# Gathers on GpSimd: one wait a block for the landing of the 15 fixed gathers, in place of waits for PE's lookups and second FFN layer

## The reference, cut to what matters

```python
n = x.shape[0]
xp = (x @ W).reshape(n, H, C)                      # H = 4 heads, C = 64
a_src = jnp.einsum('nhc,hc->nh', xp, att_src)
a_dst = jnp.einsum('nhc,hc->nh', xp, att_dst)
alpha = leaky_relu(a_src[src] + a_dst[dst], 0.2)   # one per edge and head
ex = jnp.exp(alpha - amax[dst])
w = ex / segment_sum(ex, dst)[dst]
msg = xp[src] * w[..., None]                       # the rows that are gathered
agg = segment_sum(msg, dst)
x = x + elu(agg.reshape(n, H * C) + bias)
...
h = gelu(sel @ w1 + b1); y = (h @ w2 + b2) * w_sel # FFN, of layernorm(x)
```

## Time and profile before

| | |
|---|---|
| time, median of 3 runs | 2211.67 us (2209.64 to 2214.61) |
| span of the profiled execution | 2573.5 us |
| POOL busy | 1554.5 us (60%), 1,626 instructions |
| of it the gathers (L692) | 1512.9 us, 1,563 of 968 ns on average |
| PE busy | 1981.2 us (77%) |
| DVE busy | 1581.4 us (61%) |
| ACT busy | 744.5 us (29%) |
| DMA engines, mean over the span | 143 GB/s |

### The profile page before, as it was taken

How to read it: one execution, slowest core, us unless ns; L and a number is a source line. 1 busy time by engine, 2 the same in 40 slices (tenths; PEclk the granted TensorE clock), 3 DMA queues, 4 the chain that set the end, 5 groups by cost and what they waited for, 6 DMA issues and landing times.

```text
span 2573.5 us, 29095 instructions
## 1 busy us (share of the span) xinstructions
PE 1981.2 (77%) x9511; PEld 1633.8 (63%) x9512; DVE 1581.4 (61%) x3510; ACT 744.5 (29%) x1478; POOL 1554.5 (60%) x1626
## 2 busy tenths in 40 slices
PE   8935877877877877878778877877777777877787
PEld 6723666666666666666666666666666666666666
DVE  4555655665655655656656665666665665666576
ACT  4512222222322222322232232232232232223223
POOL 2366666666666666666666666666666666666630
PEclk9967988888888889889888888988988988889889
DMA  8844444444444444444444444444444444444447
GB/s 287 276 143 121 123 134 124 132 138 120 137 138 118 132 135 124 135 140 120 134 137 128 130 136 124 134 134 130 128 134 131 127 139 124 131 136 136 119 159 312
DMA packets 157137, 369.12 MB, mean 143 GB/s; under 512 B 46646, under 2 KB 73682, under 8 KB 155699
## 3 DMA queue, kind: packets, MB, share of 16 engines
q0 software_dynamic: 75088, 208.19, 30.1%
q1 hardware_dynamic: 74706, 145.62, 16.9%
q10 hardware_dynamic: 7184, 13.41, 1.4%
HBM read 328.20 MB, written 38.89 MB: 143 GB/s over the span
## 4 chain that ended last, share of the span: by engine, by line
POOL 38%; issue 23%; PE 19%; another core or an unknown queue 9%; DVE 3%; DMA 3%; ACT 2%; POOLq 1%; DVEq 0%; SPq 0%; ACTq 0%
POOL rows L692 38%; PE ag_ps L1057 7%; PE h_ps L1021 4%; PE ag_ps L934 3%; PE y_ps L1040 3%; DMA rows<-node_rows,ends 3%; POOLq L402 1%; DVE oh L1366 1%; DVE rows L1404 1%; ACT hT L808 1%; PE ag_ps L1128 0%; ACT L808 0%; PE ag_ps L1129 0%; ACT L812 0%
## 5 line engine op out<-in xcount | busy, mean ns | idle before, releaser
L692 POOL DMA_INDIRECT rows<-node_rows,ends x1563 | 1512.9, 968 | 850.6 <-issue 482.5
L1057 PE MATMUL ag_ps<-rows,oh 128*128 128x260 f32 x3518 | 845.9, 401 | 47.5 <-DVE rows L1404 34.8
L1021 PE MATMUL h_ps<-xnT,w1s 128*128 128x256 f32 x1568 | 534.0, 500 | 419.2 <-DVE zz L1385 227.1
L1057 PEld LDWEIGHTS ag_ps<-rows,oh 128*128 128x128 f32 x3518 | 716.7, 204 | 180.3 <-DVE rows L1404 37.8
L1021 PEld LDWEIGHTS h_ps<-xnT,w1s 128*128 128x128 f32 x1568 | 377.0, 250 | 517.9 <-DVE zz L1385 234.8
L1404 DVE TENSOR_TENSOR rows<-rows,xl_ps 128x512 f32<-128x512 f32 (+3 forms) x392 | 503.1, 1346 | 47.2 <-issue 26.5
L1385 DVE TENSOR_TENSOR zz<-rows,edge_dm 128x72 f32<-128x72 f32 x98 | 22.9, 233 | 695.0 <-DMA rows<-node_rows,ends 656.4
L1040 PE MATMUL y_ps<-w2s,hT 128*128 128x256 f32 x1568 | 368.0, 386 | 12.2 <-DVE oh L1366 9.2
L831 ACT COPY rows<-rows 128x780 f32<-128x780 f32 x97 | 81.6, 842 | 998.6 <-DMA rows<-node_rows,ends 998.6
L1040 PEld LDWEIGHTS y_ps<-w2s,hT 128*128 128x128 f32 x1568 | 301.7, 194 | 66.7 <-DVE oh L1366 16.6
L1366 DVE TENSOR_TENSOR oh<-xl_ps,dloc 128x2304 f32<-128x2304 f32 x98 | 249.0, 2541 | 0.0
(11 more groups left out here) (243 smaller groups left out, 1433.7 us busy)
## 6 DMA issues: line engine op xcount, KB each, us to landing
dbc<-dst SPq DMA_DIRECT2D x97, 576.0 KB
rows<-node_rows,ends POOLq DMA_INDIRECT x1563
selfr<-node_rows SPq DMA_DIRECT2D x98, 130.0 KB
base<-in_x SPq DMA_DIRECT2D x14, 896.0 KB, 7.1
base<-in_x SPq DMA_DIRECT2D x49, 256.0 KB
ffn_rows<-yb ACTq DMA_DIRECT2D x48, 256.0 KB
node_rows<-base SPq DMA_DIRECT2D x13, 910.0 KB, 5.7
base<-in_x_turned SPq DMA_DIRECT2D x14, 384.0 KB, 7.7
```

The lines of the kernel that those rows point to most:

```text
L692: pool.indirect_dma_start(out=rows[:, b, t, :], out_offset=None, in_=table, in_offset=bass.IndirectOffsetOnAxis(ap=ends[:, b, t, 0:1], axi ...
L1021: last = nc.tensor.matmul(h_ps[:, m * PAIR:(m + 1) * PAIR], w1s[:, c, n * P:(n + 1) * P], xnT[:, c, :], start=(c == 0), stop=(c == DC - 1))
L1057: product = nc.tensor.matmul(ag_ps[b][:, 0:ROW], oh[:, b, t, :], rows[:, b, t, :], start=(t == 0), stop=False)
```

## The change

POOL no longer waits for lk_ok after four gathers, and no longer for y_ok behind the carry. It gets one new wait, all_landed: behind the 15 fixed gathers of blocks 1 to 96 and ahead of the wait for the carry, until all 15 have landed. Beside that, some values read from win are now loaded with instructions that check their bounds: the entries 1 to 4 of win, which the program that ran reads only ahead of the block loop, and DVE's count of optional landings (optional_landed), once a block.

```diff
-    LOOKED_UP, SUMMED, SECOND_LAYER = 4, (8, 11, 13), TILES - 2
+    SUMMED = (8, 11, 13)
     COLS = 8
+    WAITED_FOR = (1, 2, 3, 4)
...
         def entry(eng, w, k, most):
-            return nc.s_assert_within(eng.value_load(win[0:1, bass.ds(COLS * w + k, 1)]), 0, most,
+            at = win[0:1, bass.ds(COLS * w + k, 1)]
+            if k in WAITED_FOR:
+                return eng.value_load(at, min_val=0, max_val=most)
+            return nc.s_assert_within(eng.value_load(at), 0, most,
...
         def optional_landed(eng, w):
-            landed = eng.value_load(win[0:1, bass.ds(COLS * w + 7, 1)])
...
+            return eng.value_load(win[0:1, bass.ds(COLS * w + 7, 1)], min_val=16, max_val=16 * (NW + 3))
...
             def follow(w, started):
 
-                if started == LOOKED_UP:
-                    wait_apart(pool, (lk_ok, w + 1))
                 for k in range(GROUPS):
                     if started == SUMMED[k]:
                         wait_apart(pool, (freed[k], w))
-                if started == SECOND_LAYER and known(w, 5) and not (isinstance(w, int) and w == NW - 1):
-                    wait_apart(pool, (y_ok, w - 4))
+
+            def all_landed(w, i, b):
+
+                if not (isinstance(w, int) and w == NW - 1):
+                    wait_apart(pool, (gath[b], 16 * (TILES - 3) * (i + 1)))
...
                 if known(w, 1):
 
+                    all_landed(w, i, b)
                     wait_apart(pool, (carry_ok, w))
-                    follow(w, TILES - 2)
```

More of the change, by code:

```diff
@@ L401, in entry @@
         def entry(eng, w, k, most):
-            return nc.s_assert_within(eng.value_load(win[0:1, bass.ds(COLS * w + k, 1)]), 0, most,
+            at = win[0:1, bass.ds(COLS * w + k, 1)]
+            if k in WAITED_FOR:
+                return eng.value_load(at, min_val=0, max_val=most)
+            return nc.s_assert_within(eng.value_load(at), 0, most,
                                       skip_runtime_bounds_check_because="the window table holds counts and places of the edges' tiles, which lie within their number")
         def optional_landed(eng, w):
-            landed = eng.value_load(win[0:1, bass.ds(COLS * w + 7, 1)])
-            return nc.s_assert_within(landed, 16, 16 * (NW + 3), skip_runtime_bounds_check_because="a parity's first node block has one gather or more, each later one two at most")
+            return eng.value_load(win[0:1, bass.ds(COLS * w + 7, 1)], min_val=16, max_val=16 * (NW + 3))
         def all_extra(eng):
```

## The result

The changed kernel takes 2488.52 us (median of 4 runs, 2485.92 to 2493.59), the kernel before in the same comparison 2210.65 us (4 runs, 2208.52 to 2214.61). The ratio is 1.1262, 95% interval 1.1243 to 1.1282: slower by 278 us. The forecast was 2,450 us with a range of 2,380 to 2,505 us. The direction, the place and the range held; the forecast itself lies 38 us low. The profiled execution took 2485.92 us.

The account below looks back on a forecast made before the run. POOL issuing gathers back to back was taken as the bound. The new wait adds 2.49 us a block (2.56 + 1.18 in place of 1.25), 239 us over 96 blocks: 2211.67 + 239 = 2,451, forecast 2,450 us, range 2,380 to 2,505 us.

Parts of the forecast that it names:

- POOL's gathers bound the kernel, back to back: On POOL: 1,563 gathers at 1.273 us each, plus both ends, give 2,213 us, against the timed median of 2211.67 us.
- The late signals of PE are the cost of recording it: POOL's long waits on PE in the earlier profile, 362 us of excess span, come from recording PE's many instructions.
- The removed waits: 0: On POOL: dropping the waits for lk_ok and y_ok gains 0 in timed runs, at most 39 us.
- Landing, 2.56 us: On POOL at the new wait: the data has landed 2.56 us after the 15th gather's start.
- Restart, 1.18 us: On POOL behind the new wait: load and branch, 1.18 us from the wait's end to the next gather's start.
- Checks on DVE: 0: On DVE once a block: two checking instructions, about 0.28 us with gaps, hidden under other waiting; 27 us if all uncovered.
- The first, that the new wait takes the place of the old: On POOL: the pause shortens real old waits; about 2,212 us, or 2,330 us with half shortened; 9 in 100.
- The second: On POOL: landing already come at the wait, removed waits were the distance to the floor; 2,173 to 2,207 us; 4 in 100.
- the third, the loop through PE: From zz through PE's sums and freed[0] to POOL: 22.0 us a block, 2,591 us if PE slows a third; 7 in 100.
- What was said of the profile: POOL stands about 2.8 us ahead of the load, 270 us in 96 places, landing named; span 2,480 to 2,640 us.

Follow-up runs that it names:

- checks-only kernel: The kernel before with only the loads that check their bounds added, old waits kept, no new wait: 2216.06 us, ratio 1.0025.
- The experiment with the load ahead of the wait: The changed kernel with the entry of win read before POOL waits for the 15 landings, not behind: 2460.91 us, ratio 1.1133.
- the removals alone: The changed kernel without its wait for the 15 landings; old waits removed, checks kept: 2209.87 us, ratio 1.0003.
- the wait alone: The kernel before with the checks and the new wait added, the old waits for lk_ok and y_ok kept: 2486.37 us, ratio 1.1255.
- the kernel with two stops: The changed kernel with a further wait in each block, behind the eighth gather for those eight landings: 2715.76 us, ratio 1.2289.

## Why the prediction was right, and where not

**POOL's gathers bound the kernel, back to back.** Right. The spans of the kernels without the pause, 2215.0 us and 2208.0 us, stand beside a sum of 2,213 us; their POOL idles for little but the usual gaps; and each stop that was added is found in the time in full (276, 120 and 227 us).

**The late signals of PE are the cost of recording it.** This step fell, although what was drawn from it held (the time of the timed runs has no room for these waits). The checks-only kernel records as many instructions of the same kinds, keeps the waits for lk_ok and y_ok, and has a span of 2215.0 us without one of the waits of 3 us. If recording PE cost 362 us, it would have cost it there as well. The long waits belonged to one execution. What slowed that one stays open; so does whether the block that the prediction cites from the Trainium skill ("NOTIFIC — the notification-queue block", section 7.1) has a part in it, since no run here shows that block. That the record itself was disturbed can be read off it. The trace of before holds 12,565 signals of semaphores, 8,851 of them of DMAs; that of the checks-only kernel holds 38,242 and 32,714. The signals of the lookups are all in both, and came 2.1 us after the work in the median in the one, 0.014 us in the other: PE's signals were late there, and most of the others are missing. One sign of it was on the page of before: its list of DMA issues gives no time to landing for the gathers, which that of after puts at 2.8 us:

```profile
rows<-node_rows,ends POOLq DMA_INDIRECT x1563
```

**The removed waits: 0.** Right against the kernel before: 1.0003 [0.9992, 1.0014] without them and without the new wait (beside the checks they cost the 6 us told above); and the new wait costs the same with them (2486.37 us) as without (2488.52 us).

**Landing, 2.56 us.** This is the term that was mis-sized. Over the 96 blocks of the kernel after, the time from the start of the fifteenth gather to the landing is 2.95 us in the mean, 2.83 us in the median, with 14 blocks over 3.2 us and one of 4.45 us, which the timeline of after shows (ACT's copy starts 0.02 us after the landing):

```profile
1311.20 1.09 POOL L696 DMA_INDIRECT rows<-node_rows,ends  x1 [0.30 <-issue]
...
1315.68 0.84 ACT L835 COPY rows<-rows 128x780 f32<-128x780 f32 x1 [9.23 <-DMA rows<-node_rows,ends]
1316.81 0.94 POOL L696 DMA_INDIRECT rows<-node_rows,ends  x1 [4.52 <-issue]
```

The sum took 2.56 us from one link of the chain of waits. 0.39 us x 96 = 37 us, and the forecast's 239 us of cost fell short of the measured 278 us by 39 us. The better row stood two lines below the one that was used: in the earlier trace rows ACT, which waits for this landing, starts its copy at 1433.08 us, 2.81 us after the gather's start at 1430.27 us. What a waiting engine does tells when the signal reached it; the link of the chain is inferred from the signals on record, and of those of the fixed gathers the trace of before has 5,582 where that of after has 23,434. None of the 96 landings of the kernel after is under 2.71 us, so that the 2.56 us, and the 2.48 us of the earlier trace rows, are most likely too short. With 2.81 us, and the tail left out, the sum would have been 2,475 us. The Trainium skill, "DMA: Bandwidth & Descriptors", section "Anatomy of one DMA", by which the prediction estimated 2.31 us, is further off: the shortest of the 96 took 2.71 us, the median 2.83 us.

**Restart, 1.18 us.** Right: 1.13 us from ACT's copy in the first block shown, and from the landing 1.16 us in the mean over the 81 blocks with an optional gather. The 15 blocks without one take 1.50 us, the few tenths that the prediction left in its range. The experiment with the load ahead of the wait takes the load's 0.29 us out of it.

**Checks on DVE: 0.** Right in the two kernels that carry them without the old waits (2209.87 and 2209.53 us). In the kernel that keeps the old waits the time is 0.25% up, 6 us, and its waits for y_ok ahead of the load account for it (7.7 us). Why the kernel before, which has the same waits and no checks, does not take these 6 us was not told apart. It is no part of the 278 us, since the removals alone, with the same checks, stand at the time of before.

**The rivals.** The first, that the new wait takes the place of the old, needed 2.5 us of old waits a block; the checks-only kernel has 7.7 us of them in all, 0.08 us a block, and the wait alone cost all of the 277 us. The second needed a landing within the issue of 0.95 us; the rows have 2.8 us. For the third, the loop through PE, POOL would have had to wait at freed[0]; its waits on PE's sums come to 17.4 us in 57 places, none above 0.3 us. PE did pause longer in each block and its granted clock did fall. But the 3.78 us that the prediction took for the eight matmuls of h_ps were already their time at the lower clock. In the kernel after they take 3.45 us in the mean over 91 blocks and 3.78 us at most (2.55 us in the mean in the checks-only kernel); from zz to freed[0] it is 6.89 us in the mean, where the prediction took 4.06 + 2.98 = 7.04 us. None of the margin of 0.8 us was used up there. And with two stops, where the clock fell further, the time is still the sum of the stops. DVE's idle time ahead of zz is put to gathers, as was expected: in the row of the group all but 0.7 of 678.1 us,

```profile
L1389 DVE TENSOR_TENSOR zz<-rows,edge_dm 128x72 f32<-128x72 f32 x98 | 22.8, 233 | 678.1 <-DMA rows<-node_rows,ends 677.4
```

**What was said of the profile.** The pause came where it was expected, a little longer (3.02 us for 2.8). It was not named as a landing but as "issue"; the landing is named only where no load stands between, and not always there (the second stop: in 37 of 96 blocks). The span was to grow by less than the time; it fell by 89 us, from 2573.5 to 2484.1 us, because the span of before held 362 us that were not the kernel's. That statement rested on the step that fell; that 2484.1 us lie between the 2,480 and 2,640 us that were stated is luck.

## What to carry to other kernels

A wait for its own DMAs on the engine that issues them back to back costs the landing of the last one and the instructions that restart the stream, less what that engine has still queued in between. Here the same wait cost nothing behind the optional gathers and four more, 1.14 us a block behind one gather, and 2.82 us behind none, where a load and a branch follow it. And before a profiled execution is read for its waits, its span is to be set against the timed median: here 14% of the span were waits for which the time of the timed runs has no room.

## What was not expected of the hardware

- One profiled execution of the kernel before was 362 us longer than its timed runs, with POOL held until 10 us after the work on PE that it waited for the earlier trace rows, and two thirds of the signals missing from its trace. None of the eight profiled executions after it shows that. The cause is open.
- The landing of a gather of 128 rows of 1,040 bytes has a tail: 2.8 us in the median, over 3.2 us in 14 of 96 blocks, 4.45 us at most. Each stop pays for the mean, not for the median.
- The longer the stream stops, the lower PE's mean granted clock, without PE setting the time. Right behind the pause shown for the kernel after, from 1272.25 to 1276.10 us, the granted clock is 0.50, the level of 1.2 GHz, after PE stood idle for 4.86 us; the eight h_ps take 3.78 us. In a block of the checks-only kernel PE stood for 1.62 us, the clock from 1098.65 to 1100.65 us is 1.00, the level of 2.4 GHz, and the eight take 1.99 us:

```profile
1272.27 3.78 PE L1025 MATMUL h_ps<-xnT,w1s 128*128 128x256 f32 x8 [4.86 <-DVE zz L1389]
```

```profile
1098.66 1.99 PE L1023 MATMUL h_ps<-xnT,w1s 128*128 128x256 f32 x8 [1.62 <-DVE zz L1387]
```

The stretch of 250 to 2,050 us of the checks-only kernel and of the kernel after, and 250 to 2,000 us of the kernel with two stops (stretch and its length, then busy time and instructions of PE, PEld, DVE, ACT and POOL, granted clock as a share of 2.4 GHz, DMA share, GB/s):

```profile
250.00:2050.00 1800.00, 1553.61 (x8000) 1265.27 (x7999) 1305.49 (x2695) 594.64 (x1145) 1360.87 (x1414) 0.96 0.54 154
```

```profile
250.00:2050.00 1800.00, 1431.43 (x7014) 1196.45 (x7013) 1154.60 (x2364) 523.54 (x1010) 1196.65 (x1243) 0.88 0.48 136
```

```profile
250.00:2000.00 1750.00, 1271.97 (x6179) 1069.36 (x6180) 1019.61 (x2085) 464.26 (x893) 1063.13 (x1100) 0.84 0.43 124
```

PE is busy for 86%, 80% and 73% of these stretches, and the granted clock, a mean over its two levels of 2.4 and 1.2 GHz, goes 0.96, 0.88, 0.84. The group that pays is h_ps, whose eight matmuls after zz stand right behind the pause: same order of kernels, busy time, mean ns of one, idle time ahead of it and its releasers.

```profile
L1023 PE MATMUL h_ps<-xnT,w1s 128*128 128x256 f32 x1568 | 442.3, 431 | 255.1 <-DVE zz L1387 196.9 <-DVE dbc L1357 57.8
```

```profile
L1025 PE MATMUL h_ps<-xnT,w1s 128*128 128x256 f32 x1568 | 523.8, 493 | 448.7 <-DVE zz L1389 426.0 <-DVE dbc L1359 21.7
```

```profile
L1027 PE MATMUL h_ps<-xnT,w1s 128*128 128x256 f32 x1568 | 545.6, 509 | 652.1 <-DVE zz L1391 638.0 <-DVE dbc L1361 13.5
```

From 0.431 to 0.493 to 0.509 us each, while the sums (ag_ps) went from 0.395 to 0.401 us and stayed there. The time follows POOL alone all the same.
